# Second cross attention: a pair's residual and normalisation on ScalarE and GpSimd instead of VectorE, and VectorE's copies of turned probabilities moved behind the maximum

## The reference

```
def _L1_xattn_ref(x, context, ln_gamma, ln_beta, w_q, w_kv, w_out, b_out, gate):
    xn = _layernorm(x, ln_gamma, ln_beta)
    q = (xn @ w_q).reshape(B, SQ, 16, 64)
    k, v = jnp.split(context @ w_kv, 2, axis=-1)          # 16 heads of 64
    scores = jnp.einsum('bqhd,bkhd->bhqk', q * SCALE, k)
    attn = jax.nn.softmax(scores, axis=-1)
    out = jnp.einsum('bhqk,bkhd->bqhd', attn, v).reshape(B, SQ, INNER)
    return (out @ w_out + b_out) * jnp.tanh(gate[0])
...
x = _layernorm(x + _L1_xattn_ref(x, ctx_1024, ...), axis=-1)
```

## Time and profile before

| | us |
|---|---|
| median of 3 runs | 1885.1 (1882.76 to 1885.45) |
| profiled execution, its own time | 1884.88 |
| profiled execution, span | 1883.0 |
| PE busy in the span | 1667.1 (89%) |
| DVE busy | 1549.9 (82%) |
| ACT busy | 1275.3 (68%) |
| POOL busy | 925.5 (49%) |

### The profile page before, as it was taken

The page is one execution under the profiler, slowest core; times in us unless marked ns, Lnnn a source line. Parts: engine busy times, 40 slices in busy tenths (PEclk is TensorE's granted clock), DMA queues, the critical chain, the costliest instruction groups (busy, mean ns, idle before and its releaser), DMA issues. The chain is left out here.

```text
span 1883.0 us, 34675 instructions
## 1 busy us (share of the span) xinstructions
PE 1667.1 (89%) x10425; PEld 1009.4 (54%) x10425; DVE 1549.9 (82%) x2885; ACT 1275.3 (68%) x2106; POOL 925.5 (49%) x723
## 2 busy tenths in 40 slices
PE   4987996889957899999999999999999999994997
PEld 2654665777733344554554554454455455454886
DVE  2765785877758999999999999999999999975887
ACT  2442332877735887887888788788788888864554
POOL 3640111363335766565665656656567465421333
PEclk9997998799978999999999999999999999997998
DMA  5203884311100898988899898898888889973231
GB/s 190 95 0 127 306 332 173 85 42 45 45 34 17 180 197 174 199 182 179 190 183 190 183 190 187 178 195 182 179 199 179 188 183 185 182 135 122 47 79 29
DMA packets 632266, 281.85 MB, mean 150 GB/s; under 512 B 601852, under 2 KB 606236, under 8 KB 631452
## 3 DMA queue, kind: packets, MB, share of 16 engines
q1 hardware_dynamic: 632204, 281.10, 64.2%
HBM read 129.02 MB, written 1.05 MB: 69 GB/s over the span
## 5 line engine op out<-in xcount | busy, mean ns | idle before, releaser
L2237 DVE SCALAR_TENSOR_TENSOR xa_h<-xa_psum,xa_rinv,xa_h 128x500 f16<-128x500 f32 x672 | 452.8, 730 | 1.0 <-ACT xa_h L2445 0.7
L2445 ACT ACTIVATE xa_h<-xa_psum,xa_rinv 128x1000 f16<-128x1000 f32 x448 | 371.5, 883 | 51.8 <-DVE xa_rinv L2228 51.5
L2429 ACT ACTIVATE xa_psum<-xa_psum,xa_bias,unscale_s 128x1500 f32<-128x1500 f32 x224 | 353.2, 1577 | 7.4
L2073 PE MATMUL xa_psum<-xa_c_hi,xa_q_hi 128*128 128x500 f16 x672 | 257.4, 383 | 54.5 <-DVE xa_h L2237 50.1
L2217 DVE TENSOR_REDUCE xa_psum<-xa_psum 128x1 f32<-128x1000 f32 x224 | 269.3, 1202 | 14.2 <-PE xa_psum L2075 13.4
L2098 PE MATMUL xa_psum<-xa_prT,xa_n_hi 128*128 128x512 f16 (+1 forms) x768 | 270.8, 353 | 3.6 <-issue 1.6
L2100 PE MATMUL xa_psum<-xa_prT,xa_n_lo 128*128 128x512 f16 (+1 forms) x768 | 270.6, 352 | 0.0
L2099 PE MATMUL xa_psum<-xa_prT,xa_n_hi 128*128 128x512 f16 (+1 forms) x768 | 270.6, 352 | 0.0
L2074 PE MATMUL xa_psum<-xa_c_lo,xa_q_hi 128*128 128x500 f16 x672 | 252.7, 376 | 0.0
L2075 PE MATMUL xa_psum<-xa_c_hi,xa_q_lo 128*128 128x500 f16 x672 | 252.4, 376 | 0.0
L1939 POOL TENSOR_SCALAR xa_ctxT<-xa_ctxT,scales 128x1500 f32<-128x1500 f32 x31 | 126.3, 4073 | 166.4 <-DMA xa_ctxT<-in_ctxT 166.4
(11 more groups left out here) (328 smaller groups left out, 3630.4 us busy)
## 6 DMA issues: line engine op xcount, KB each, us to landing
ctxN<-in_ctxP SPq DMA_DIRECT2D x16, 1536.0 KB, 9.5
xa_ctxP<-in_ctxP SPq DMA_DIRECT2D x32, 768.0 KB, 4.3
ctxT<-in_ctxT SPq DMA_DIRECT2D x16, 1500.0 KB, 6.4
xa_ctxT<-in_ctxT SPq DMA_DIRECT2D x32, 750.0 KB, 4.7
moe_spread<-weight_rows SPq DMA_DIRECT2D x16, 1024.0 KB, 8.4
xa_prT<-xa_h SPq DMA_TRANSPOSE x192, 5.5
up<-in_F_up SPq DMA_DIRECT2D x1, 2048.0 KB, 7.7
down<-in_F_down SPq DMA_DIRECT2D x1, 2048.0 KB, 11.8
```

The source lines that it names most:

```text
L2073: nc.tensor.matmul(out, qh, c_hi[:, b, a:z], start=True, stop=False)
L2237: nc.vector.scalar_tensor_tensor(low, psum[:, bank + a:bank + z, 0:W], rinv[:, s % 2, :], high, ALU.mult, ALU.subtract).then_inc(h2_ready, 1)
L2429: nc.scalar.activation(psum[:, bank:bank + 3, 0:W], psum[:, bank:bank + 3, 0:W], ACT.Exp, bias=bias[:, s % 2, :], scale=k.unscale_s[:, :], ...
L2445: nc.scalar.activation(h[:, H_SLOT[s], 0, a * W:z * W].rearrange("p (a c) -> p a c", c=W), psum[:, bank + a:bank + z, 0:W], ACT.Identity, ...
```

## The change

DVE loses `residual`, the moments and the normalisation. ACT gets three short instructions on 128x128 elements: `sum_x` (step 7) sums the rows of xg, `gate` (step 9) writes y * tanh(gate) with its row sums, `square` (step 11) sums the squares of r minus the mean. POOL gets the rest: r = yg + xg and the negated mean (`residual`), and, in `normalise`, the variance plus epsilon, the power of minus one half, the normalised tokens and their store. In POOL's order `gated` moves ahead of `scale_c(i+1, 0)`, `residual` stands where the tail stood, and `normalise` comes behind `scale_c(i+1, 1)`. PE's second round of unit 4 waits for `yg_ready` instead of `t.r_ready`, that is for the read of bank 7 by ACT instead of DVE. DVE's `keep_turned` moves from ahead of `maximum(s)` to behind it.

The core of the diff:

```diff
@@ POOL
                 pool.wait_ge(bias_ready, 1)
                 pool.wait_ge(t.r_ready, last(i))
+                pool.sem_inc(gating, 1)
+                pool.wait_ge(x_sum_ready, last(i))
                 pool.tensor_tensor(xg[:, :, :], k.x_tok[:, bass.ds(i, 1), :], gated_bias[:, :].unsqueeze(1), ALU.add)\
                     .then_inc(xg_ready, 1)
+
+            def residual(i):
+
+                pool.wait_ge(yg_ready, this(i))
...
+                pool.tensor_tensor(t.r[:, :, :], yg[:, :, :], xg[:, :, :], ALU.add).then_inc(t.r_ready, 1)
+                pool.wait_ge(x_sum_ready, this(i))
+                pool.sem_inc(gating, 1)
+                pool.tensor_scalar(neg_mean[:, :], y_sum[:, :], x_sum[:, :], -1.0 / D, ALU.add, ALU.mult)\
+                    .then_inc(neg_mean_ready, 1)
+
+            def normalise(i):
+
+                pool.wait_ge(squares_ready, this(i))
...
+                pool.tensor_scalar(t.var_eps[:, 0, :], squares[:, :], 1.0 / D, k.eps[:, :], ALU.mult, ALU.add)\
+                    .then_inc(t.var_eps_ready, 1)
+                pool.wait_ge(t.var_eps_ready, this(i))
...
+                pool.tensor_tensor(t.rstd[:, 0, :], t.var_eps[:, 0, :], k.minus_half[:, :], ALU.pow).then_inc(t.rstd_ready, 1)
+                pool.wait_ge(t.rstd_ready, this(i))
...
+                pool.tensor_scalar(t.xn[:, 0, :], t.r[:, 0, :], neg_mean[:, :], t.rstd[:, 0, :], ALU.add, ALU.mult)\
+                    .then_inc(t.xn_ready, 1)
+                t.pool_store(pool, i, 0)
...
                 split_n(i, 0, first)
+                if not first:
+                    gated(i - 1)
                 if not end:
                     scale_c(i + 1, 0)
...
                 split_n(i, 1)
                 if not first:
-                    gated(i - 1)
-                    t.pool_rstd(pool, i - 1, 0)
-                    t.pool_store(pool, i - 1, 0)
+                    residual(i - 1)
                 if not end:
                     scale_c(i + 1, 1)
+                if not first:
+                    normalise(i - 1)
@@ PE
                 if u == TURNED[0] and r == 1 and not first:
-                    pe.wait_ge(t.r_ready, this(i - 1))
+                    pe.wait_ge(yg_ready, this(i - 1))
@@ DVE
                 if s or not first:
                     inverse(*unit(i, s - 1))
+                maximum(i, s)
                 at = turn_at(*unit(i, s - 1))
                 if at and (s >= UPS or not first):
                     keep_turned(*at)
-                if s == RESIDUAL and not first:
-                    residual(i - 1)
-                maximum(i, s)
...
-                if not first:
-                    if s == NORMALISE:
-                        t.vector_normalise(dve, i - 1, 0)
@@ ACT
+                nc.scalar.activation(yg[:, 0, :], xg[:, 0, :], ACT.Identity, accum_out=x_sum[:, :]).then_inc(x_sum_ready, 1)
...
+                nc.scalar.activation(yg[:, 0, :], psum[:, 7, 0:128], ACT.Identity, scale=k.gate_tanh[:, :],
+                                     accum_out=y_sum[:, :]).then_inc(yg_ready, 1)
...
+                nc.scalar.activation(yg[:, 0, :], t.r[:, 0, :], ACT.Square, bias=neg_mean[:, :],
+                                     accum_out=squares[:, :]).then_inc(squares_ready, 1)
...
             def step(i, s, first=False, end=False):
                 exponentials(i, s)
+                if s == min(OUTPUT) and not first:
+                    sum_x(i - 1)
+                if s == max(OUTPUT) and not first:
+                    gate(i - 1)
+                if s == SQUARES and not first:
+                    square(i - 1)
```

More of the change, by code:

```diff
@@ L1671, in state_cross_phase @@
     FIRST_BANKS = (0, 1, 2, 3)
[L1672 removed]
+    PROJECT, OUTPUT, SQUARES, STORE, LOGITS = {2: 0, 3: 1, 4: 2, 5: 3}, {7: 0, 8: 1, 9: 2}, 11, 12, 13
     OUTPUT_HEADS = (0, 6, 11, H1)
@@ L1734, in state_cross_phase @@
         on = sb("on", [128, H1, 2, SP])
-        gated_bias, xg = sb("gated_bias", [128, D]), sb("xg", [128, 1, D])
+        gated_bias, xg, yg = sb("gated_bias", [128, D]), sb("xg", [128, 1, D]), sb("yg", [128, 1, D])
+        y_sum, x_sum, neg_mean, squares = (sb(n, [128, 1]) for n in ("y_sum", "x_sum", "neg_mean", "squares"))
         psum = ctx.enter_context(nc.psum_tensor("xa_psum", [128, 8, 512], fp32))
@@ L1752, in state_cross_phase @@
         on_zeroed, y_ready, bias_ready, xg_ready = sem("on_zeroed"), sem("y_ready"), sem("bias_ready"), sem("xg_ready")
+        yg_ready, x_sum_ready, sum_ready = sem("yg_ready"), sem("x_sum_ready"), sem("sum_ready")
+        neg_mean_ready, squares_ready, gating = sem("neg_mean_ready"), sem("squares_ready"), sem("gating")
         two_ready = sem("two_ready")
@@ L1864, in _ @@
             t.open_pool(pool)
+            open_sems(pool, 1, t.r_ready, t.xn_ready, neg_mean_ready)
             open_sems(pool, 1, xg_ready)
@@ L1911, in gated @@
                 pool.wait_ge(t.r_ready, last(i))
+                pool.sem_inc(gating, 1)
+                pool.wait_ge(x_sum_ready, last(i))
                 pool.tensor_tensor(xg[:, :, :], k.x_tok[:, bass.ds(i, 1), :], gated_bias[:, :].unsqueeze(1), ALU.add)\
                     .then_inc(xg_ready, 1)
+            def residual(i):
+                pool.wait_ge(yg_ready, this(i))
+                pool.sem_inc(gating, 1)
+                pool.wait_ge(squares_ready, last(i))
+                pool.sem_inc(gating, 1)
+                pool.wait_ge(t.xn_ready, last(i))
+                pool.tensor_tensor(t.r[:, :, :], yg[:, :, :], xg[:, :, :], ALU.add).then_inc(t.r_ready, 1)
+                pool.wait_ge(x_sum_ready, this(i))
+                pool.sem_inc(gating, 1)
+                pool.tensor_scalar(neg_mean[:, :], y_sum[:, :], x_sum[:, :], -1.0 / D, ALU.add, ALU.mult)\
+                    .then_inc(neg_mean_ready, 1)
+            def normalise(i):
+                pool.wait_ge(squares_ready, this(i))
+                pool.sem_inc(gating, 1)
+                pool.wait_ge(t.rstd_ready, last(i))
+                pool.sem_inc(gating, 1)
+                pool.tensor_scalar(t.var_eps[:, 0, :], squares[:, :], 1.0 / D, k.eps[:, :], ALU.mult, ALU.add)\
+                    .then_inc(t.var_eps_ready, 1)
+                pool.wait_ge(t.var_eps_ready, this(i))
+                pool.sem_inc(gating, 1)
+                pool.wait_ge(t.xn_ready, last(i))
+                pool.tensor_tensor(t.rstd[:, 0, :], t.var_eps[:, 0, :], k.minus_half[:, :], ALU.pow).then_inc(t.rstd_ready, 1)
+                pool.wait_ge(t.rstd_ready, this(i))
+                pool.sem_inc(gating, 1)
+                pool.wait_ge(t.xnT_ready, last(i))
+                pool.sem_inc(gating, 1)
+                pool.wait_ge(t.tok_stored, last(i))
+                pool.sem_inc(gating, 1)
+                pool.tensor_scalar(t.xn[:, 0, :], t.r[:, 0, :], neg_mean[:, :], t.rstd[:, 0, :], ALU.add, ALU.mult)\
+                    .then_inc(t.xn_ready, 1)
+                t.pool_store(pool, i, 0)
             def split_q(i, b):
@@ L1998, in _ @@
             gated(PAIRS - 1)
-            t.pool_rstd(pool, PAIRS - 1, 0)
-            t.pool_store(pool, PAIRS - 1, 0)
+            residual(PAIRS - 1)
+            normalise(PAIRS - 1)
         @block.tensor
@@ L2198, in epilogue @@
                     outputs(i, part)
-                pe.wait_ge(t.r_ready, this(i))
+                pe.wait_ge(yg_ready, this(i))
                 t.tensor_transpose(pe, i, 0, psum[:, 7, 128:256])
@@ L2210, in _ @@
             open_sems(dve, NR, *turn_kept.values())
-            t.open_vector(dve)
+            open_sems(dve, 1, t.logits_kept)
             def maximum(i, s):
@@ L2245, in keep_turned @@
                     turn_bank).then_inc(turn_kept[u], 1)
[L2247 to L2253, removed]
             def step(i, s, first=False, end=False):
@@ L2382, in epilogue @@
                 keep_turned(i, TURNED[1], 2)
-                residual(i)
-                t.vector_normalise(dve, i, 0)
                 t.vector_logits(dve, i, 0, psum[:, 7, 0:E])
@@ L2394, in _, with sum_x, gate, square @@
             open_sems(act, NG, on_kept)
+            open_sems(act, 1, x_sum_ready, yg_ready, squares_ready)
             t.open_scalar(act)
+            def sum_x(i):
+                act.wait_ge(xg_ready, this(i))
+                act.wait_ge(squares_ready, last(i))
+                act.wait_ge(neg_mean_ready, last(i))
+                nc.scalar.activation(yg[:, 0, :], xg[:, 0, :], ACT.Identity, accum_out=x_sum[:, :]).then_inc(x_sum_ready, 1)
+            def gate(i):
+                act.wait_ge(y_ready, this(i))
+                act.wait_ge(x_sum_ready, this(i))
+                nc.scalar.activation(yg[:, 0, :], psum[:, 7, 0:128], ACT.Identity, scale=k.gate_tanh[:, :],
+                                     accum_out=y_sum[:, :]).then_inc(yg_ready, 1)
+            def square(i):
+                act.wait_ge(t.r_ready, this(i))
+                act.wait_ge(neg_mean_ready, this(i))
+                act.wait_ge(t.var_eps_ready, last(i))
```

(5 more changed lines are left out.)

## The result

The changed kernel is slower: 1903.4 us median (1900.7 to 1907.0, 6 runs) against 1883.4 (1881.3 to 1885.5, 6 runs) for the kernel before in the same comparisons, a ratio of 1.0108 with a 95% interval of 1.0092 to 1.0123. That is 20 us, inside the stated range of 1878 to 1910 and on the forecast side, but twice the forecast's +10. The profiled execution took 1906.4, its span 1904.4 us.

The account below looks back on a forecast made before the run. Bound: the loop maximum, bias, exp, inverse in plain steps, PE in steps 7 to 9. Sum: 14 pairs at +0.68 (9.5), last window -0.6, first pair's copies -0.2, tail +1.4, so +10.1: 1895 us, range 1878 to 1910.

Parts of the forecast that it names:

- Step 10 gives 0.57, not 1.1: Residual and moments leave DVE: max(10) moves 0.57 us earlier, the rest of the stall becoming a wait for PE.
- PE's own step that was to give 0.04 back: PE's step 10 takes 4.45 us against 4.41, so 0.04 of the saving is lost again.
- A copy step saves 0.08: Copies behind the maximum save 0.08 us of DVE's wait for ACT in each of steps 0, 1, 2, 11, 12.
- The 0.10 given back in 13 to 0: Between max(13) and max(0), PE's step 13 leaves 4.51 us instead of 4.41, losing 0.10.
- step 2 was costed at nothing: PE's projection in step 2 waits for a copy of the same step; that was claimed to cost nothing.
- Step 7 was costed at a loss of 0.25: In step 7 the later copy delays PE's output product, which shares its bank: 0.25 us lost.
- The stall costs 1.26: Step 12: PE's token transpose waits for POOL's normalisation, queued behind a scaling that waits for DMA: 1.26 us a pair.
- The 0.12 that I had added for step 13: From the late max(13) to max(0), PE's 4.63 us counts instead of 4.51: 0.12 more in the stall.
- ACT's three instructions cost nothing: ACT's added instructions, 0.27 us each between exp and the high part, are covered by its wait: cost 0.
- the serial chain behind the last pair: Behind the loop, the serial tail grows from 2.3 us to about 3.7: +1.4.
- the third rival: Square between exps makes ACT load tables twice a pair, steps 11 and 12: +31 us, about 1926; chance 0.04.
- The first rival: Tokens ready by 1068.2, so step 12 has no stall: -7.5 us in sum, 1877; chance 0.14.

Follow-up runs that it names:

- e1: The changed kernel with POOL's normalise put ahead of scale_c(i+1, 1), directly behind residual; 1876.4 us, ratio 0.9962 to the kernel before.
- e5: e1 with the copy of step 7 alone ahead of the maximum again; 1870.9 us, ratio 0.9930 to the kernel before.
- e7: The changed kernel with an unused 128x512 copy on POOL at the head of normalise, behind the scaling; 1917.7 us, ratio 1.0181 to the kernel before.
- e2: The changed kernel with DVE's copies ahead of the maximum again, the tail as changed; 1904.2 us, ratio 1.0114 to the kernel before.

## Why the prediction was right in kind and half too small

The first three sentences in bold are terms of the prediction; what was measured for each follows.

**Step 10 gives 0.57, not 1.1.** Measured 9 to 10: 5.53 to 4.96, 0.57 exactly, and max(10) now waits 0.49 us for PE:

```profile
1063.89 1.21 DVE L2260 TENSOR_REDUCE xa_psum<-xa_psum 128x1 f32<-128x1000 f32 x1 [0.49 <-PE xa_psum L2118]
```

PE's own step that was to give 0.04 back did not (10 to 11: 4.40).

**A copy step saves 0.08.** It saves 0.18 to 0.20 (4.81 or 4.82). I had left DVE a part of the 0.16 as a distance between two instructions; the whole 0.16 of waiting and some more goes. The 0.10 given back in 13 to 0 came (4.53). But step 2 was costed at nothing, and 2 to 3 takes 5.12 instead of 4.82: 0.3 lost, PE's projection behind the copy and then the maximum waiting 0.31 for the scores. Step 7 was costed at a loss of 0.25 against a step without a copy; 6 to 8 went from 9.65 to 10.06, 0.41. Sum of these parts without the stall, read from e1: 66.77 against 67.51, -0.74, forecast -0.58.

**The stall costs 1.26.** It is there, in the place and by the queue that was named, in the 14 pairs that have a scaling between; the first pair and the last have none (4.7 us from 12 to 13 in both). Its size is the term that was mis-sized: 68.57 against e1's 66.77 is 1.80 a pair. PE's idle stretch ahead of the transpose, foreseen at about 1.5, is 2.2 to 2.9. In the pair shown, the tokens came 13.82 behind max(10) (1063.89 to 1077.71), forecast 13.51: the load reached POOL 4.79 behind its issue instead of 4.57, and POOL's chain took 1.87 instead of 1.78, since it waits 0.18 and 0.41 between its instructions where I had 0.08, while the tokens themselves took 0.44 instead of 0.7. The scores then started 0.28 behind the tokens instead of 0.45; the 0.18 in it was a guess that no row showed. The larger part is on the other side: steps 10 to 12 got shorter than forecast, so that max(13) would have come 14.02 behind max(10) (4.40 + 4.81 + 4.81 in e1) and not 14.29. That makes 1.55 for this pair (15.57 - 14.02) against 1.14. Its step 12 to 13 of 6.36 is 0.19 short of the median, mostly because its load came early: over the 14 pairs the scaling starts 4.71 to 5.48 behind the load's issue, 4.94 in the median, and 4.80 here. The 0.12 that I had added for step 13 didn't come (4.53 with and without the stall). What is won in steps 10 to 12 only makes PE arrive earlier at a wait whose end is fixed by the DMA: the load is issued 8.05 behind max(9) before and after (1050.99 to 1059.04, 1058.93 to 1066.98). Neither the residual's departure nor the copies can be worth anything there as long as the stall stands.

**The clock and the end.** Two more terms were missing or too small. Granted clock: the two pairs with a stretch at 1.2 GHz in the profiled execution are 3.9 us longer together than the median pair; I took PE's stall for its own length only. And the serial chain behind the last pair: forecast +1.4 from the output product to the tokens. It went from 2.3 to 4.2 us (1719.66 to 1723.82), +1.9:

```profile
1719.66 0.37 ACT L2437 ACTIVATE xa_yg<-xa_psum,gate_tanh 128x128 f32<-128x128 f32 x1 [3.64 <-PE xa_psum L2176]
...
1723.37 0.45 POOL L1952 TENSOR_SCALAR xa_xn<-xa_r,xa_neg_mean,xa_rstd 128x128 f32<-128x128 f32 x1 [0.40 <-POOL xa_rstd L1945]
```

**The sum again, with what was measured.** From the first maximum of the sublayer to that of the last step the profiled executions take 1072.7 and 1089.5 us: +16.8. Behind it +2.9, and ahead of it +1.7, in phases that the change doesn't touch; the first maximum lay anywhere from 600.3 to 606.1 us in the profiled executions of the different kernels, so this last part is not the change's. 16.8 + 2.9 is the measured 20. In the 16.8 the 14 pairs have 17.6 where 9.5 was forecast, and the first pair gives 0.8 back where I had 0.2. The last pair was to give 0.6 and gives nothing as far as its last maximum (60.40 before, 60.38 after).

**ACT's three instructions cost nothing, and no tables are loaded.** In e5 the distances 7 to 8 and 8 to 9, in and behind the step with `sum_x`, are 4.63 and 4.96 as before; in e1 11 to 12 and 12 to 13, in and behind the step with `square`, take 4.81 like 0 to 1 and 1 to 2, which have none. The groups by line for ACT in the changed kernel: 0.30, 0.36 and 0.39 us, 0.19 to 0.20 for each read, and the six table loads of before. The Trainium skill (ScalarE: Activation LUTs, "What ACT_TABLE_LOAD costs") gives 186 ns plus 0.833 ns an element, and 93 more for each operand by pointer; for 128 elements that is an estimate of 293 and 386. The trace agrees for `sum_x` with 297 and for `square` with 390; `gate`, which has a pointer too and reads PSUM, took 357, 29 less. The 1.28 us loads that the third rival feared didn't come.

**The first rival** (tokens in time, 1877) did not happen in the changed kernel, but e1 built its condition and measured 1876.4. That the number fits is partly luck: up to the last maximum e1's profiled execution gained 11.3 us where 8.9 was forecast, and behind it lost 3.2 where 1.4 was forecast.

## What to carry to other kernels

When work is moved to an in-order queue, ask not how busy the engine is but what stands ahead of the work in that queue and what that waits for: POOL was 50% idle, and the step still took 1.7 us more than with the tokens in time, because the tokens stood behind an instruction that waited for a DMA. Put what someone waits for ahead of what waits. Gains ahead of a wait whose end is fixed elsewhere are not gains, so a step's saving is to be read at the next point where all the engines meet. And moving a copy behind a reduction is worth its overlap only where the engine that needs the copy in the same step does not become the late one by it. In steps 2 and 7 it does: PE's projection and its output product wait for the copy (the projection 0.45 us a pair in the changed kernel), and the next maximum waits for PE. In the other four PE waits for the copy by 0.2 us at most, ahead of the turn's and the tokens' transposes, and the step is still 0.2 shorter.

## What the runs showed of the hardware beyond that

PE's stall has a second price. The granted clock fell to its lower level (1.2 GHz; the window shows a mean of 0.55) beside idle stretches ahead of the token transpose of 2.67 and 2.88 us in two pairs of the changed kernel, of 2.61 to 3.23 in six of e7, and of 2.32 to 3.17 in three of e2. It did not fall with the other twelve of the changed kernel, up to 2.60, nor with eight of e7, up to 3.07. So the length of the stretch alone does not decide it, and what does stays open. Such a pair is 1.5 to 2 us longer in the changed kernel and in e7.

GpSimd was not slow at this work: 128x128 elements with two operations and two scalars by pointer took 0.44 us beside 0.34 on DVE (L296 before), 1.3 times, where the one-operation row of before had 0.618. What cost time on POOL were the gaps between three dependent instructions, 0.18 and 0.41 us, where 0.08 stood before between L274 and L279. Before, two semaphore waits and nothing else stand between the two; now it is two waits and an increment, and in the second gap three of each. That the gaps come from the increments is not shown.
